# A gated cross-attention and FFN block: first loads on one queue in order of need, top rows rooted alone, other rows' statistics joined by two small products, first queries in three batches

## The reference

```python
x = x + jnp.tanh(g_xattn[0]) * _L0_xattn_ref(_layernorm(x), ctx_1024, ctx_1024, 0, mask_SxS2_ff0)
x = x + jnp.tanh(g_ffn[0]) * _L0_ffn_ref(_layernorm(x), Wq, Wr, aux_keys, aux_values, Wvd, Wvu, Wu1, ...)

def _layernorm(x, axis=-1, eps=1e-05):
    m = jnp.mean(x, axis=axis, keepdims=True)
    v = jnp.var(x, axis=axis, keepdims=True)
    return (x - m) / jnp.sqrt(v + eps)

# _L0_xattn_ref, x (8, 224, 2048): 32 heads of 64 share 8 groups of keys, 750 keys each
scores = jnp.einsum('bsgrd,btgd->bgrst', xq, xk) / math.sqrt(64)
scores = scores + mask
probs = jax.nn.softmax(scores, axis=-1)
out = jnp.einsum('bgrst,btgd->bsgrd', probs, xv)
# _L0_ffn_ref: a router over 512 slots (top 8), and a gate from a 2048 -> 512 -> 1 network
```

## Time and profile before

| | |
|---|---|
| median of 3 runs | 1227.89 us |
| profiled execution | 1228.12 us, its span 1226.3 us |
| TensorE busy | 1175.6 us (96%), 14638 products |
| VectorE, ScalarE, GpSimd busy | 985.6, 890.6, 896.1 us |
| transferred | 94.71 MB, mean 77 GB/s |
| granted clock of TensorE | 0.997 of full |

### The profile page before, as it was taken

One profiled execution on the slowest core, in us unless ns is written; L12 is line 12 of the kernel. 1 busy time (PEld: TensorE's weight loads), 2 busy tenths in 40 slices (PEclk: granted clock), 3 DMA queues, 4 the chain that ended last, 5 costly groups with the idle time before them and its releaser, 6 DMA issues.

```text
span 1226.3 us, 35213 instructions
## 1 busy us (share of the span) xinstructions
PE 1175.6 (96%) x14638; PEld 914.5 (75%) x14638; DVE 985.6 (80%) x2217; ACT 890.6 (73%) x1207; POOL 896.1 (73%) x837
## 2 busy tenths in 40 slices
PE   1999999999999999999999999999999999999997
PEld 0788888888888888888888888888877555555553
DVE  2898899889889988998898889888883776666564
ACT  2888888888888888888888888888861355444443
POOL 1899999999999999999899998999870023121313
PEclk9999999999999999999999999999999999999999
DMA  7412132131213222221312231131226200121112
GB/s 248 166 34 81 53 98 75 40 96 48 79 42 91 59 71 58 78 82 45 98 34 81 57 94 40 41 76 49 68 90 229 104 1 1 70 103 74 65 70 103
DMA packets 60289, 94.71 MB, mean 77 GB/s; under 512 B 35746, under 2 KB 44962, under 8 KB 55908
## 3 DMA queue, kind: packets, MB, share of 16 engines
q1 hardware_dynamic: 59700, 89.87, 23.4%
q10 hardware_dynamic: 432, 2.59, 0.6%
HBM read 71.36 MB, written 20.97 MB: 75 GB/s over the span
## 4 chain that ended last, share of the span: by engine, by line
PE 80%; ACT 8%; DVE 6%; POOL 2%; issue 2%; DMA 1%; SPq 0%; DVEq 0%; POOLq 0%
PE psum L773 13%; PE psum L796 13%; PE psum L849 11%; PE psum L803 7%; PE psum L784 6%; PE psum L826 6%; PE psum L820 5%; PE psum L821 5%; PE psum L920 3%; ACT arena L631 2%; ACT arena L627 2%; PE psum L755 2%; PE psum L836 2%; DVE arena L1115 2%; PE psum L864 2%
## 5 line engine op out<-in xcount | busy, mean ns | idle before, releaser
L519 POOL TENSOR_TENSOR arena<-arena 128x768 bf16<-128x768 f32 x448 | 652.0, 1469 | 61.3 <-ACT arena L627 44.2
L1115 DVE CUSTOM_DVE_ANT_0 arena<-psum,arena 128x750 f32<-128x750 f32 x448 | 420.1, 938 | 82.7 <-PE psum L784 75.4
L631 ACT ACTIVATE arena<-arena,neg_max 128x750 f32<-128x750 f32 x448 | 410.6, 917 | 64.6 <-DVE neg_max L1115 64.6
L627 ACT ACTIVATE arena<-psum 128x768 f32<-128x768 f32 x320 | 258.2, 807 | 64.8 <-PE psum L803 62.5
L773 PE MATMUL psum<-arena 128*128 128x512 bf16 x896 | 272.1, 384 | 1.6 <-DVE arena L1130 1.6
L796 PE MATMUL psum<-ident,arena 128*128 128x128 f32 x1792 | 268.3, 272 | 0.0
L820 PEld LDWEIGHTS psum<-arena 128*128 128x128 bf16 (+1 forms) x2688 | 194.6, 98 | 57.5
L821 PE MATMUL psum<-arena 128*128 128x64 bf16 (+1 forms) x2688 | 222.0, 193 | 0.0
L820 PE MATMUL psum<-arena 128*128 128x65 bf16 (+1 forms) x2688 | 221.7, 194 | 0.0
L821 PEld LDWEIGHTS psum<-arena 128*128 128x128 bf16 (+1 forms) x2688 | 178.5, 98 | 53.2
L796 PEld LDWEIGHTS psum<-ident,arena 128*128 128x128 f32 x1792 | 206.1, 140 | 4.3
(11 more groups left out here) (131 smaller groups left out, 1433.4 us busy)
## 6 DMA issues: line engine op xcount, KB each, us to landing
arena<-in_k_t SPq DMA_DIRECT2D x128, 187.5 KB, 3.2
out<-arena SPq DMA_DIRECT2D x13, 1024.0 KB, 3.9
arena<-in_v_rows SPq DMA_DIRECT2D x64, 192.0 KB, 2.4
arena<-in_x_top SPq DMA_DIRECT2D x7, 1024.0 KB, 6.4
arena<-in_x_rest SPq DMA_DIRECT2D x8, 768.0 KB, 4.9
spill<-arena SPq DMA_DIRECT2D x96, 64.0 KB, 2.2
arena<-spill SPq DMA_DIRECT2D x6, 1024.0 KB, 6.8
arena<-in_w_t SPq DMA_DIRECT2D x4, 1024.0 KB, 13.6
```

The costliest lines, as they stand in the source:

```text
L519: pool.tensor_tensor(p_lo[:, n % RING, :], p_sb[:, n % RING, :], high(p_sb[:, n % RING, :]), ALU.subtract).then_inc(p_split, 1)
L627: act.activation(p_sb[:, n % RING, :], flat_ps[:, turned_at(n):turned_at(n) + CW], ACT.Copy).then_inc(evac_a, 1)
L631: act.activation(s_sb[:, n % RING, 0:CTX], s_sb[:, n % RING, 0:CTX], ACT.Exp, bias=neg_max[:, n % 4, :], scale=-1.0).then_inc(exped, 1)
L1115: dve.tensor_tensor_reduce(s_sb[:, n % RING, 0:CTX], flat_ps[:, score_at(n):score_at(n) + CTX], mask_sb[:, max(n % UNITS - REP + 1, 0), :] ...
```

## The change

- SyncE's queue takes the first loads in a new order: the top rows of entry 0 in four pieces of 512 columns with a semaphore each, the other rows, K of group 0, the mask of the top rows (one of its four blocks), V of group 0, the rest of the mask. ScalarE's queue keeps the gate. The gather and the spread of entry 0 are gone; those of the later entries stay.
- VectorE takes the top rows' statistics first. GpSimd's root and factors for entry 0 run once on the top column alone and once on the other three.
- The other rows' statistics of entry 0 are joined on TensorE. `quad` is a 128x128 matrix with 1/4 where two partitions hold the same row. One product with the four parts' means gives their mean on every partition; VectorE adds to each part's variance its squared distance from that mean, and a second product gives the variance.
- The first pair's seven transposes come in three batches (two, three, two) instead of two: two of top rows before everything else, three of other rows, two of top rows.
- For entry 0, ScalarE normalises only the first 128 columns of each block of other rows, and inside the loop; GpSimd does the other 384 (L564 of the changed kernel).
- GpSimd splits K of group 0 between the two roots, not behind both.

```diff
@@ -378,7 +399,7 @@
                     sp.dma_start(gathered[:, :, r, :], stats_rest[QUAD * r:QUAD * r + QUAD]).then_inc(rest_gathered, 16)
 
             def spread_rest(b):
-                sp.wait_ge(rest_merged, b + 1)
+                sp.wait_ge(rest_merged, b)
                 for r in range(REP):
                     sp.dma_start(ln_mv[QUAD * r:QUAD * r + QUAD, 1:1 + NB, :], mv_rest[:]).then_inc(rest_spread, 16)
 
@@ -390,11 +411,13 @@
                         sp.dma_start(spill[at:at + QUAD].rearrange("i (g r d) -> i g r d", g=KV, r=REP)[:, :, r, :],
                                      xb[QUAD * r:QUAD * r + QUAD, b % 3, j].rearrange("i (g d) -> i g d", g=KV)).then_inc(spilled[b % 3], 16)
 
+            for c in range(4):
+                sp.dma_start(xa[:, 0, 512 * c:512 * c + 512], x_top[0, :, 512 * c:512 * c + 512]).then_inc(first_top_loaded[c], 16)
             load_rest(0)
             load_k(0)
+            sp.dma_start(mask_sb[:, 0:1, :], mask[:, 0:1, :]).then_inc(mask_loaded, 16)
             load_v(0)
-            gather_rest(0)
-            spread_rest(0)
+            sp.dma_start(mask_sb[:, 1:1 + NB, :], mask[:, 1:1 + NB, :]).then_inc(mask_rest_loaded, 16)
             load_k(1)
             load_v(1)
             load_top(1)
...
+            def root(i, cols):
+
+                if i == 0:
+                    pool.wait_ge(top_merged, 1)
+                elif i == 1:
+                    pool.wait_ge(rest_joined, 1)
+                else:
+                    pool.wait_ge(rest_spread, 16 * REP * (i - 1))
+                    pool.wait_ge(top_merged, i)
+                pool.tensor_tensor(ln_ve[:, cols], ln_mv[:, cols, 1], ln_eps[:, cols], ALU.add).then_inc(ln_ve_done, 1)
+                pool.wait_ge(ln_ve_done, i + 1)
+                pool.tensor_tensor(ln_rstd[:, cols], ln_ve[:, cols], ln_half[:, cols], ALU.pow).then_inc(ln_rstd_done, 1)
...
-            root(0)
-            factors(0)
+            whole = slice(0, 1 + NB)
+            top_col, rest_cols = slice(0, 1), slice(1, 1 + NB)
+            root(0, top_col)
+            factors(0, top_col)
+            split_k(0)
+            root(1, rest_cols)
+            factors(1, rest_cols)
+            pool.wait_ge(ln_done, 2)
+            for j in range(NB):
+                pool.tensor_scalar(xn_rest[:, j, 2 * D:], xb[:, 0, j, 2 * D:], ln_scale[:, 1 + j:2 + j], ln_bias[:, 1 + j:2 + j],
+                                   ALU.mult, ALU.add).then_inc(rest_widened, 1)
```

ScalarE and TensorE (the rest of the diff moves waits to the new counts):

```diff
-            act.dma_start(xa[:, 0, :], x_top[0]).then_inc(top_loaded[0], 16)
             act.dma_start(tanh_gx[:, :], g_x).then_inc(gx_loaded, 16)
-            act.dma_start(mask_sb[:, :, :], mask).then_inc(mask_loaded, 16)
...
             def norm_rest(b, j):
-                act.wait_ge(ln_done, b + 1)
-                act.activation(xn_rest[:, j, :], xb[:, b % 3, j, :], ACT.Identity, bias=ln_bias[:, 1 + j:2 + j],
+                act.wait_ge(ln_done, b + 2)
+                cols = slice(0, KV * D if b else 2 * D)
+                act.activation(xn_rest[:, j, cols], xb[:, b % 3, j, cols], ACT.Identity, bias=ln_bias[:, 1 + j:2 + j],
                                scale=ln_scale[:, 1 + j:2 + j]).then_inc(rest_normed, 1)
...
+            def round_first(i):
+                for half in range(2):
+                    round_q(FIRST_BANK[i], 0, half, FIRST_TURNS[i], i + 1)
+
             norm_top(0)
-            for j in range(NB):
-                norm_rest(0, j)
+            round_first(0)
...
+                if m in (3, 4) and 1 <= pair < PAIRS:
+                    round_q((window + 1) % 2, pair, m - 3, turn_range(window), window + 4)
+                if k == -4:
+                    for j in range(NB):
+                        norm_rest(0, j)
+                if k in (-3, -2):
+                    round_first(k + 4)
...
+            def turn_first(i):
+                pe.wait_ge(top_normed, 1)
+                if i == 1:
+                    pe.wait_ge(rest_normed, NB)
+                if i == 2:
+                    pe.wait_ge(q_split, 2)
+                turn_rows(0, FIRST_TURNS[i], FIRST_BANK[i])
+
...
+                    pe.wait_ge(q_split, queries_before(pair) + m + 1)
+                if pair == 0 and (g, m) == (0, REP):
+                    pe.wait_ge(q_split, 3)
+                if pair == 0 and g == 1 and m in (0, 1):
+                    pe.wait_ge(q_split, 5 + m)
+                if pair > 0 and (g % 2, m) in ((0, UNITS - 1), (1, 1)):
+                    pe.wait_ge(q_split, queries_before(pair) + 3 + half)
...
+            turn_first(0)
+            pe.wait_ge(quad_set, 1 + REP)
+            pe.wait_ge(own_merged, 1)
+            pe.matmul(psum[:, 5, 0:NB], quad[:, :], own_mv[:, :, 0], start=True, stop=True).then_inc(own_averaged, 1)
+            pe.wait_ge(own_step, 3)
+            pe.matmul(psum[:, 3, 0:NB], quad[:, :], own_sum[:, :], start=True, stop=True).then_inc(own_spread, 1)
...
-                if m == 2 and 0 <= window // 2 + 1 < PAIRS:
+                if m == 2 and 1 <= window // 2 + 1 < PAIRS:
                     turn_q(window)
+                if k in (-3, -2):
+                    turn_first(k + 4)
```

VectorE:

```diff
+            def split_first(i):
+                for half in range(2):
+                    split_q(FIRST_BANK[i], 0, half, FIRST_TURNS[i], 2 * i + half + 1)
+
             for c in range(4):
                 top_stats(0, c)
             merge_top(0)
-            merge_rest(0)
+            for j in range(NB):
+                rest_stats(0, j)
+            dve.wait_ge(rest_summed, 1)
+            for j in range(NB):
+                ins = dve.bn_aggr(own_mv[:, j, :], stats_rest[:, j, :])
+            ins.then_inc(own_merged, 1)
+            dve.wait_ge(own_averaged, 1)
+            dve.tensor_tensor(own_dev[:, :], own_mv[:, :, 0], psum[:, 5, 0:NB], ALU.subtract).then_inc(own_step, 1)
+            dve.wait_ge(own_step, 1)
+            dve.tensor_tensor(own_sq[:, :], own_dev[:, :], own_dev[:, :], ALU.mult).then_inc(own_step, 1)
+            dve.wait_ge(own_step, 2)
+            dve.tensor_tensor(own_sum[:, :], own_sq[:, :], own_mv[:, :, 1], ALU.add).then_inc(own_step, 1)
+            dve.tensor_copy(ln_mv[:, 1:1 + NB, 0], psum[:, 5, 0:NB])
+            split_first(0)
+            dve.wait_ge(own_spread, 1)
+            dve.tensor_copy(ln_mv[:, 1:1 + NB, 1], psum[:, 3, 0:NB]).then_inc(rest_joined, 1)
             dve.wait_ge(mask_loaded, 16)
             dve.wait_ge(gx_tanh, 1)
...
+                if n == REP:
+                    dve.wait_ge(mask_rest_loaded, 16)
```

124 lines of the change are left out of this document (73 added, 51 removed).

## The result

| | before | after |
|---|---|---|
| median of 6 runs of each | 1228.07 us (1226.64 to 1229.98) | 1218.23 us (1214.72 to 1220.6) |
| profiled execution | 1228.12 us, span 1226.3 | 1217.31 us, span 1215.1 |

After over before is 0.9917, with a 95% interval of 0.9901 to 0.9934: 9.8 us faster. The forecast was 1215.3 with a range of 1213.4 to 1219.5; the time lies 2.9 above the forecast and inside the range.

A forecast was written before the change was run, and what follows sets the result against it. The prediction took TensorE's chain, 80% of the span, as the bound, with only its start movable. Gain min(13.3, 12.6) = 12.6 from 1228.12 gave 1215.5, less 0.2 for the median: 1215.3 us, range 1213.4 to 1219.5.

The forecast's parts named there:

- The bound: Whole kernel: TensorE's long chain is untouched; only its start, and lateness of something it needs later, can change.
- Rivals C: Whole kernel: no change, something fixed in time rather than the opening sets the steady part; 1228 us, chance 0.02.
- D: Transfers: slower, one queue alone carries 11.8 MB at 210 GB/s, k(2) lands at 59.4; 1237 us, chance 0.03.
- Landing of the first loads: Opening loads: top rows' last quarter lands at 6.85, other rows at 8.85 as now, bounds 7.4 and 10.6.
- Rival B: Opening: 2 KB pieces at 210 GB/s land other rows at 10.6, batches add 3.3; gain 9.9, 1218 us, chance 0.18.
- Top rows alone: Opening: top rows' statistics end at 7.7, ScalarE starts at 9.5, top queries ready for VectorE at 11.4.
- Joining: Other rows by two tiny products: stands ahead of VectorE's first subtraction; first score at 13.1, 15.0 earlier.
- K's split as cover: GpSimd, opening: K of the first group lands about 10.5, is split at 12.0, so just covered.
- What the opening pays back: First score to first V product: new work adds 1.7 to 9.06; first V product at 23.8, 13.3 earlier.
- The cap: Third group's K, k(2): lands at 37.4, GpSimd waits 1.3, so the gain cannot exceed 12.6.
- Its own sign of being wrong: First eight units: wrong if their time changes by over 0.7, or first-V-product and end shifts differ over 2 us.
- The sum: Whole kernel: gain is the smaller of opening shift 13.3 and k(2) limit 12.6, giving 1215.3 us.

The follow-up runs named there:

- e3: Changed kernel plus 67 idle identity products on TensorE in the opening, 56 of them ahead of the first transposes; 1222.16 us.
- e5: Changed kernel with both GpSimd roots waiting for the joined statistics, K split behind both, small products before transposes, joining before first subtraction; 1225.02 us.
- e6: Changed kernel with the two small products replaced by gather, merge and spread by DMA, on ScalarE's queue; 1239.74 us.
- e7: Changed kernel with VectorE's first subtraction ahead of the joining steps and TensorE's second small product behind the first score; 1217.44 us.
- e8: e1 with both small products ahead of the first transposes and VectorE's first subtraction behind the joined variance; 1216.85 us.
- e9: Changed kernel with e1's single load, e4's weight order, and the first small product ahead of the transposes, second behind; median 1216.88 us, ratio 0.9908.
- e1: Changed kernel with the top rows of entry 0 in one load instead of four pieces, same SyncE queue; 1215.70 us.
- e2: Changed kernel with the four top-row pieces issued on ScalarE's queue instead of SyncE's; 1218.25 us.
- e4: Changed kernel with first FFN weights and router weights loaded behind K of the third group, k(2); 1216.70 us.
- e10: e9 plus 41 idle identity products on TensorE, 36 of them ahead of the first small product; median 1214.23 us, ratio 0.9891.
- e11: e10 with the top rows in two loads of 4 KB rows instead of one; 1214.67 us.
- e12: The changed kernel, unedited, profiled and run once more; median 1217.27 us, ratio 0.9915.

## Why the spans differ by 11.2 and the medians by 9.8

The shift is 9.69 from 44 us to the last score reduction near 906 us, and 11.29 at the first tile of the FFN. The 1.6 between come from the kernel before. Its windows, and those of the same work in the changed kernel:

```profile
915.00:918.00 3.00, 0.86 (x12) 0.68 (x10) 2.78 (x12) 1.09 (x2) 0.00 (x0) 1.00 0.17 53
918.00:921.00 3.00, 2.79 (x8) 0.81 (x9) 2.67 (x6) 1.00 (x2) 0.00 (x0) 0.67 0.47 99
921.00:924.00 3.00, 3.00 (x12) 1.16 (x11) 2.31 (x5) 0.71 (x2) 0.49 (x2) 0.76 0.49 104
```

```profile
906.00:909.00 3.00, 0.65 (x8) 0.42 (x4) 2.82 (x11) 0.41 (x1) 0.00 (x0) 1.00 0.22 34
909.00:912.00 3.00, 3.00 (x13) 1.04 (x12) 2.67 (x6) 1.71 (x3) 0.00 (x0) 1.00 0.63 97
```

Both kernels leave TensorE idle for some 2 us at the passage to the FFN. In the profile of before the granted clock then averages 0.67 and 0.76, a stretch at the lower level of 1.2 GHz; in that of after it stays at 1.00. The router's pair of products (64x512) takes 1.77 in the one and 1.06 in the other. The stretch is in the profiles of before, e3, e5, e6, e7, e8 and e9 and not in those of after, e1, e2, e4, e10, e11 and e12. That the 1.6 is the stretch is shown: in e7 and e8, which have one of the same length, the shift stays within 0.03 across this passage (11.21 to 11.18, 11.76 to 11.74), while in e1 and e4, which have none, it grows by 1.4 and 1.6. None of the kernels touches the FFN, so I take the stretch for chance and not for an effect of the change. The runs of one kernel speak for that: the six of e9 have a mean granted clock of 0.995 to 0.998, and the time goes with it (1217.19 to 1220.29 at 0.995, 1214.65 and 1214.1 at 0.998 and 0.997). It is not proved, since no kernel was profiled both with the stretch and without it. The medians cannot decide: 9.84 between before and after is close to 9.69, but 10.95 between before and e12 is close to 11.3.

## Why the prediction held, and where it did not

- **The bound.** Right. TensorE follows its own pace behind the opening, and the shift made there arrives at the end of the attention unchanged. Rivals C (no change) and D (one queue at 210 GB/s) are out: from 14 to 20 us the one queue moved 278 GB/s, and k(2) was there by 40.23.
- **Landing of the first loads: mis-sized, and the main miss.** The term said 8.85 for the other rows, "because the same bytes on two queues did that", and the test in the text was "if the other rows' statistics start after 10, B". They started at 11.00. The 210 GB/s of the first 5 us belonged to whole loads on two queues; with four 2 KB pieces it was 159. One queue is not the reason: with one load on it (e1) the first 5 us had 164, and the other rows still landed at 8.99. On the two queues of before the 1.84 MB were complete at 9.11, not 8.85, since the top rows came last. e1 puts the pieces' share at 1.8 us of the end (9.69 to 11.52). Rival B named the pieces as the reason and had 10.6.
- **Top rows alone.** Each step had the size given: root and factors from 8.90 to 10.57 are 1.67 (1.76 in the text), normalisation 0.81. The chain began 1.0 to 1.2 late, which was harmless.
- **Joining.** Right in mechanism: VectorE's subtraction was what the first score came behind. From the statistics' start to the first score the text had 4.25 (13.1 - 8.85) and the trace 4.32. That close a sum is part luck: the small product with its lags took 0.75 (13.22 to 13.97) where the text had 0.3, and the aggregates and small steps took less than it gave them.
- **K's split as cover.** It held: the split ended 0.3 before the subtraction began, with a wait of 2.49 on the load. Where the subtraction comes 1.4 earlier (e7) the split is the releaser. Where the loads come earlier (e1), K comes with them, its split began at 10.96, and the cover holds as well.
- **What the opening pays back.** 2.13 to the first V product and 2.74 in all (12.75 to 10.0), instead of 1.7. The second root took the joined statistics at 15.91 and ScalarE had normalised by 19.98, as late as the loads made it (17.6 in the text). e3 shows that TensorE's low pace is 2.0 of it, and that at full pace 0.7 is left. So these were two misses of opposite sign: the new work among the engines, priced at 1.7, cost about 0.7, and the pace had no term. The prediction did not read that the products of the opening in the earlier trace rows (1.01 a pair) were slow ones, of which there now are more.
- **The cap.** Right in mechanism, mis-sized again: k(2) is late for GpSimd, but it landed at 40.2, not 37.4. The formula of the text, 49.36 + 0.62 less the landing, gives 9.8 with 40.2; 9.69 was measured, and 9.67 in e12. Most of the miss is again the pieces: with the top rows in one load (e1) and nothing else changed k(2) landed at 37.36, which is the text's 37.4, though it was also issued 1.5 earlier there. So "less 6.0 for the pause that is gone" came out only for a queue that starts on time; as changed, k(2) took 8.9 from its issue, where it had taken 3.8. What it waits behind is the weights: with the 4.6 MB behind it instead of ahead (e4) it took 3.1, and GpSimd never waited. The formula that the prediction sets beside its landing times (the Trainium skill, "DMA: Bandwidth & Descriptors", section on the anatomy of one DMA) is given there for transfers that GpSimd issues; SyncE and ScalarE issue these. No term of the sum used it.
- **Its own sign of being wrong.** The first eight units were to take the time of before, 15.71, within 0.7. They took 16.63 (26.51 to 43.14), 0.92 more: 0.3 is the wait for k(2), 0.62 the rest of what the opening pays back, which fell behind the first V product. By its letter the sign was met, narrowly. The other one was not: the shift of 10.62 at the first V product and of 9.69 at the end are 0.9 apart.
- **The sum.** min(13.3, 12.6) became min(10.0, 9.7). Both terms shrank by about three, and the mechanism stayed. The pieces are in both: without them (e1) the shift is 11.52 and nothing is cut at k(2). What is left to 13.3 is the first score, 1.0 later than in the text (14.12), and 2.4 paid back there instead of 1.7. The measured gain of 9.8 lies outside the forecast's own 11.0 to 13.2; the range held because it was drawn to take in B. The time is nearer to B's 1218 than to the forecast; B had the right landing and 3.3 for the way where 2.74 were measured, for another reason than the pace, and no cap. The chance of 0.58 on the forecast's own size was too high beside B's 0.18, since the text itself listed 7.4 to 10.6 for a landing on which all else was summed.

Open: what stopped TensorE for the 1.0 of e3; why two queues served whole loads well and pieces badly; and whether the lower clock at the passage to the FFN is chance. e5 and e6 each change several things at once, so their sizes belong to the bundle.

## What to carry to other kernels

When a kernel is one long chain behind an opening, follow the chain of the opening link by link, and measure the shift at a numbered instruction rather than at the end: it told a cut of 0.3 us inside one trace, where runs of one kernel differ by 3 us. Between two traces it is only as good as the opening repeats, here 0.4. Splitting a load so that work can begin on its first piece pays only if that piece is on the deciding chain; here the load behind it was, and the pieces made it later. And when a pause in the transfers is removed, ask of every small DMA that used to run in the pause what it costs in a full queue, and of every load that used to follow the pause what now stands ahead of it.

## What the runs showed of the hardware

- The same 1 MB to 128 partitions was usable at 6.52 as one load and at 7.82 as four pieces; the next load's user began at 9.21 or 11.00. With two pieces it began at 10.55, with one load in the same kernel at 9.37.
- A gather of four small DMAs was usable 5.1 us after its first issue while only a V load and the mask were still moving, and 14.0 after it (13.07 to 27.08) behind some 7 MB of issued loads, though it was issued from another engine than they.
- TensorE's products in the opening took 1.01 to 1.06 a pair against 0.60, while the column of the granted clock read 1.00, for which the trace has no record before 24.09 (31.54 in before); products kept running from 1.5 us on (e3, e10) made the first real pair take 0.60.
- GpSimd's power of -0.5 took 0.56 for one column, 0.89 for three and 1.04 for four.
